# A selective-scan stage: stores of dl, of the C and B rows and of y begun by ScalarE instead of SyncE

## The reference, cut to what matters

```
x_dbl = einsum('bkdl,kcd->bkcl', xs, x_proj_w)      # 6 dt rows, 16 B rows, 16 C rows
delta = softplus(einsum(dts, dt_proj_w) + dt_proj_b) # 192 rows
dA = exp(delta[..., None] * A)                       # 192 channels x 16 states
h  = dA * h + (delta * u)[..., None] * B             # along the 4096 pixels
y  = einsum('bkdn,bkn->bkd', h, C)
return y + xs * Dk                                   # the four k are then added up
```

## Time and profile before

| | |
|---|---|
| time, median of 3 runs | 11577.95 us (11575.34 to 11589.02) |
| time of the profiled execution | 11574.58 us |
| its span, first to last instruction | 11572.8 us |
| granted TensorE clock, mean | 0.957 |
| DVE busy | 10116.4 us (87%) |
| ACT busy | 8511.6 us (74%) |
| POOL busy | 9157.8 us (79%) |
| data moved | 1716.32 MB |

### The profile page before, as it was taken

One profiled execution on the slowest core, in us unless ns is written; L12 is line 12 of the kernel. 1 busy time (PEld: TensorE's weight loads), 2 busy tenths in 40 slices (PEclk: granted clock), 3 DMA queues, 4 the chain that ended last, 5 costly groups with the idle time before them and its releaser, 6 DMA issues. The chain is left out here.

```text
span 11572.8 us, 332532 instructions
## 1 busy us (share of the span) xinstructions
PE 9678.0 (84%) x136268; PEld 6104.2 (53%) x136268; DVE 10116.4 (87%) x6303; ACT 8511.6 (74%) x15618; POOL 9157.8 (79%) x3978
## 2 busy tenths in 40 slices
PE   8967888788888788888787778888888887999999
PEld 5644444444444444444444444444444444788778
DVE  7879999999999999999999999999999996555554
ACT  3468888887888788878888888788888884444443
POOL 1169999998999899989999999899999996433330
PEclk9989999999999999999999999999999998999999
DMA  3366676676667766776677666666766674212210
GB/s 103 106 164 169 171 175 171 167 178 168 172 166 174 177 167 164 173 174 168 171 175 178 172 167 171 175 168 171 178 174 166 171 175 111 65 48 67 61 50 12
DMA packets 561649, 1716.32 MB, mean 148 GB/s; under 512 B 147138, under 2 KB 147938, under 8 KB 558344
## 3 DMA queue, kind: packets, MB, share of 16 engines
q1 hardware_dynamic: 560136, 1695.05, 58.4%
HBM read 1319.08 MB, written 375.39 MB: 146 GB/s over the span
## 5 line engine op out<-in xcount | busy, mean ns | idle before, releaser
L975 POOL TENSOR_TENSOR HC<-H,crep 128x1024 f32<-128x1024 f32 x3072 | 7201.2, 2376 | 583.8 <-PE psum L723 416.0
L797 DVE TENSOR_TENSOR_SCAN H<-E,car,psum 128x1024 f32<-128x1024 f32 x2112 | 4868.7, 2336 | 237.4 <-PE psum L701 113.3
L701 PE MATMUL psum<-diag,dluT 128*32 128x128 f32 x98304 | 3350.7, 288 | 1083.0 <-DVE H L797 1049.2
L701 PEld LDWEIGHTS psum<-diag,dluT 128*32 128x32 f32 x98304 | 2852.9, 116 | 2080.8 <-DVE H L797 1887.9
L882 ACT ACTIVATE E<-dlr,am 128x1024 f32<-128x1024 f32 x2816 | 3194.4, 1143 | 1001.7 <-DMA dlr<-scr_dl 519.4
L866 ACT ACTIVATE diag<-idn,blt 128x128 f32<-128x128 f32 x8192 | 2521.6, 389 | 119.8 <-PE psum L701 119.8
L723 PE MATMUL psum<-HC,sely 128*32 128x512 f32 x12288 | 2232.0, 620 | 32.6 <-POOL HC L975 30.9
L775 DVE TENSOR_TENSOR psum<-dur,psum 128x1024 f32<-128x1024 f32 x1280 | 1548.7, 1210 | 114.6 <-PE psum L664 90.4
L797 DVE TENSOR_TENSOR_SCAN H<-E,psum 128x1024 f32<-128x1024 f32 x704 | 1582.1, 2276 | 75.6 <-PE psum L701 45.9
L664 PE MATMUL psum<-sx,selb 96*128 96x512 f32 x2560 | 981.4, 465 | 532.4 <-DVE H L797 522.3
L664 PEld LDWEIGHTS psum<-sx,selb 96*128 96x128 f32 x2560 | 395.4, 190 | 1423.5 <-DVE H L797 1139.3
(11 more groups left out here) (143 smaller groups left out, 9796.9 us busy)
## 6 DMA issues: line engine op xcount, KB each, us to landing
dur<-scr_dlu SPq DMA_DIRECT2D x3072, 128.0 KB, 4.0
dlr<-scr_dl SPq DMA_DIRECT2D x3072, 128.0 KB, 3.8
crep<-scr_bc SPq DMA_DIRECT2D x1024, 256.0 KB, 5.2
scr_dlu<-dlu SPq DMA_DIRECT2D x256, 384.0 KB, 4.6
scr_yk<-yt SPq DMA_DIRECT2D x256, 384.0 KB, 3.0
brep<-scr_bc SPq DMA_DIRECT2D x512, 128.0 KB, 3.5
scr_dl<-dlt SPq DMA_DIRECT2D x128, 384.0 KB, 5.6
scr_dl<-yt SPq DMA_DIRECT2D x128, 384.0 KB, 3.3
```

What stands on the lines that cost most here:

```text
L701: r = e.matmul(P[un % 2][32 * q:32 * q + 32, i * 128:(i + 1) * 128], dluT[:, m % 2, i, 32 * j:32 * j + 32], diag[:, i, at + q, :], start=T ...
L797: e.tensor_tensor_scan(H[:, un % NH, ::step], decay[:, ::step], drive[:, ::step], init, ALU.mult, ALU.add).then_inc(scan_done)
L975: e.tensor_tensor(HC[:, un % NHC, :], H[:, un % NH, :], crep[:, GREP.index(g), :], ALU.mult).then_inc(hc_done)
```

## The change

The stores of delta, of the B and C rows and of y leave SyncE's order, and ScalarE begins them, at units written out in its loop: `store_y(n - 1)` at unit 5 of every step, `out_bc(c)` at unit 6 of an even step, `out_dl(2c)` at unit 8 and `out_dl(2c + 1)` at unit 11. Each stands behind the exponential that `ahead` issues at that unit. The functions are the same, with the same waits. The stores of dlu stay on SyncE.

```diff
@@ sync
-        def out_dl(m):
...
-        def out_bc(c):
...
-        def store_y(m):
...
                 if n:
                     in_crep(c - 1, 1)
-                    store_y(n - 1)
                 load_y(n + 1)
...
-                if c < NCHUNK:
-                    out_bc(c)
                 if more:
                     in_dlr(n + 1, 2)
                     in_dur(n + 1, 2)
...
                 if n + 2 < NSTEP:
                     out_dlu(n + 2)
-                    out_dl(n + 2)
-                    out_dl(n + 3)
             else:
...
                 if n + 2 < NSTEP:
                     out_dlu(n + 2)
-                store_y(n - 1)
                 load_y(n + 1)
@@ scalar
+        def out_dl(m):
+            if m >= 4:
+                for j in range(NJ):
+                    e.wait_ge(dlr_in[slot(m - 4, j)], loaded(m - 4, j))
+            e.wait_ge(dl_made, m + 1)
+            e.dma_start(S["dl"][m % 4], dl[m % 2]).then_inc(dl_out[m % 2], 16)
+
+        def out_bc(c):
+            if c >= 2:
+                e.wait_ge(crep_in[1], 64 * (c - 1))
+            e.wait_ge(bc_copied, c + 1)
+            e.dma_start(S["bc"][c % 2], bc[NR:NR + NS + 4, :]).then_inc(bc_out, 16)
+
+        def store_y(m):
+            b, k, ci, half = steps[m]
+            t0 = t_of(k, ci)
+            e.wait_ge(y_copied, m + 1)
+            e.dma_start(S["yk"][b, k % 2, half, :, t0:t0 + TC], yt[:]).then_inc(y_stored, 16)
...
             ahead(un)
+            if n < NSTEP and n % 2 == 0 and c < NCHUNK:
+                if x == 6:
+                    out_bc(c)
+                if x == 8:
+                    out_dl(2 * c)
+                if x == 11:
+                    out_dl(2 * c + 1)
+            if x == 5 and n:
+                store_y(n - 1)
             if un % 2 == 0 and has_carry(un - 1):
                 carry(un - 1)
```

More of the change, by code:

```diff
@@ L577, in sync @@
             load_rows(0, ci)
-        out_bc(0)
         for i in range(2):
@@ L582, in sync @@
         for m in range(2):
-            out_dl(m)
             out_dlu(m)
@@ L630, in sync @@
                     in_crep(c, 0)
-        store_y(NSTEP - 1)
         e.wait_ge(y_stored, 16 * NSTEP)
@@ L912, in scalar @@
         project(0)
+        out_bc(0)
         delta(0)
+        out_dl(0)
         turn_b(0)
@@ L916, in scalar @@
         delta(1)
+        out_dl(1)
         e.wait_ge(a_made, 2)
```

## The result

The changed kernel takes 11631.8 us (median of 6 runs, 11619.4 to 11661.6) against 11578.4 us (11571.1 to 11589.0) before it: a ratio of 1.0051, 95% interval 1.0037 to 1.0066. It is slower, by 53 us; 38 were forecast. The ratio is worked out from all runs, so it is not quite that of the two medians (1.0046); its interval is 43 to 76 us. The profiled execution has a span of 11617.6 us, 44.8 more than before. It is the fastest of the six, with a mean granted TensorE clock of 0.958, where the six together have 0.955; the runs of the kernel before that were timed beside the experiments have 0.958.

A forecast was written before the change was run, and what follows sets the result against it. VectorE was taken to bound the scan, its idle time set by the landing of dlr third 0. Losses of 14 us (lines one and two) and 24 us (three and four) gave 11578 + 38 = 11616 us, range 11551 to 11700.

The forecast's parts named there:

- What bounds the scan: Scan: the change acts through VectorE's idle time; dlr third 0's landing decides, and waits beyond about 3.4 us cost nearly fully.
- Point 2: First dl store, moved ahead of dlr third 0's landing: delays it 0.8 us; 14 us lost in lines one and two, 24 later.
- Point 1, the head start: Lines three and four: without bc ahead on SyncE, dlr loads start 0.42 us earlier per pair, gaining at most 27 us.
- Point 3: ScalarE's loop: issuing the stores is hidden under the exponentials and costs nothing; if not hidden, 0.6 us per pair.
- Point 4: Second dl store and y stores: moving them, and the earlier loads for step n + 2, give nothing.
- A: Rival, critical loads: not bound by the DMA engines, so the store is free; 11551 us, -0.23%; chance 0.14.
- B: Rival, dl store: price of 0.2 to 0.6 us, half covered by slack, no change to be told; 11564 to 11598 us; chance 0.26.
- C: Rival, ScalarE: store issue not hidden, 0.6 us more on the landing; 11675 us; chance 0.13.
- D: Rival, DMA engines: the dl store is paid at the loads' rate, 1.7 us; 11710 us; chance 0.10.
- The signs: Profile: ScalarE's dlr wait up 40 to 100 us, VectorE's busy time unchanged, SyncE's L573 and L535 waits about the same.
- a sum of 52 us: DMA queues taking turns packet by packet: the dl store's full price of 0.94 us is paid, 33 + 19 = 52 us.

The follow-up runs named there:

- the two runs with nothing in the way: Changed kernel with the first dl store back on SyncE, 11572.6 us, ratio 0.9991; or at unit 10 of ScalarE's loop, 11574.2 us, ratio 0.9993.
- the two other runs that lose as much: Kernel before with only the first dl store on ScalarE at unit 8, 11641.9 us; or with it ahead of dlr third 0 on SyncE, 11638.9 us.
- the late store: Changed kernel with the first dl store at unit 10 of ScalarE's loop in place of unit 8: 11574.2 us, ratio 0.9993.

## Why the prediction was right, point by point

- **What bounds the scan.** Right. VectorE's busy time is unchanged, and all of the loss is idle time: over the first seven images, in windows, the total grew by 41.0 us (7905.80 to 7946.84) and VectorE's busy time by 2.7 (7544.86 to 7547.56). The landing of dlr third 0 was the point on which it turned: well ahead of its use, it gives 106 us; delayed by one store, it takes 53.
- **Point 2, the price of the store.** Right in place and sign, a little small in size. It was priced at 0.8 us for the landing, and at 14 us in the first two lines and, less the head start, 24 in the last two. By the windows above, scaled to 64 pairs each, it was 0.21 x 64 = 13 us and 0.58 x 64 = 37 us. The wait grew by 87 us over 128 pairs, 0.7 us each: by 1.0 in the first two lines, where most of it was covered, and by 0.66 in the last two, where nearly all of it was paid (0.58 by the windows). So 0.8 was a good mean of two different delays; it was taken as the middle of 0 and 1.7, and that it came out so well is in part luck. The store was also begun earlier than the prediction has it: not right behind the exponential of unit 10 but ahead of its start, 7.85 us before the exponential of unit 12 in place of some 5.
- **Point 1, the head start.** Wrong: it was not there to be taken off in the last two lines. It was costed at 0.42 us for each of 64 pairs, 27 us in all. With the loss undone, the head start should show: the two runs with nothing in the way gave 7.5 and 5.9 us, both with an interval that reaches 1 and whose other end, 21 and 22 us, lies under 27. Timelines show why, SyncE's first and then ScalarE's, in a pair of a fourth line, in the run with one store put back, answering to the earlier trace rows:

```profile
4009.99 0.32 SPq L562 DMA_DIRECT2D yp<-scr_yk  x1
...
4010.88 1.83 SPq L519 DMA_DIRECT2D dlr<-scr_dl  x4
...
4024.76 1.15 ACT L862 ACTIVATE E<-dlr,am 128x1024 f32<-128x1024 f32 x1 [7.43 <-DMA dlr<-scr_dl]
```

  The dlr loads start 0.89 us after yp, where it was 1.31, but the exponential starts 14.77 us after yp, where it was 14.49. The same holds over all pairs. In the fourth lines the dlr loads start 1.31 us after yp before, and 0.89 in this run (medians of 32 pairs); in the third lines there was hardly a head start at all, 0.81 and 0.71. From yp to the exponential of unit 12 it is 13.77 us before and 13.72 in this run in the fourth lines, and 11.55 and 11.65 in the third (means). The step that failed read a head start in issue as one in landing. The likely reason: yp is in the queue ahead, and in the pair of the earlier trace rows the DMA engines are busy at a share of 0.97 to 1.09 from 4004 to 4016, so the landing goes by when they begin and by how many bytes there are, not by when SyncE writes the last of them.
- **What the prediction left out: TensorE's clock.** In the windows of images 2 to 7, last two lines, the clock stands at the lower of its two levels (0.5 of full speed) for 307 to 333 us in the three profiles with the loss and for 268 to 300 us in the three without. Over the lines of these six profiles, a us at the lower level goes with a line longer by 0.19 us. By this estimate some 0.1 of the 0.73 us per pair comes with the clock. Between single runs of the kernel before it shows too: 11560.6 us at a mean clock of 0.962 and 11605.7 at 0.953. That the longer waits lower the clock is not shown.
- **Point 3, ScalarE's time at nothing.** Right. The store is issued under a running instruction, and the run with all five stores on ScalarE and this one moved to unit 10 shows no loss.
- **Point 4, nothing from the rest.** Right within the error: putting back the first dl store alone brings back the time before.
- **The rivals.** A (the store is free) falls with the changed kernel and the two other runs that lose as much; but the 313 GB/s of loads and store together, against 243 to 254 of loads alone, shows that its mechanism works in part. B (nothing to be told) falls with the interval of 43 to 76 us. C falls with the late store. D would have asked for 132 us.
- **The signs.** ScalarE's wait rose by 87 us, within the 40 to 100 named. VectorE's work is unchanged. But the prediction had SyncE's waits for yp and for the exponential remain with about their totals, and they grew by 924 and 749 us: with the stores gone, SyncE reaches these waits earlier and stands there until the same moment.
- The Trainium skill (DMA: Bandwidth & Descriptors, "Issuing engines are not separate DMA queues") was cited for transfers of different engines that interleave on the same 16 DMA engines; the runs agree, 11641.9 us from ScalarE's queue and 11638.9 from SyncE's. The turn-taking between queues that this page of the Trainium skill states ("Queues, rings and completion order") fits the 142 GB/s of the store beside 171 of the loads. It gave a sum of 52 us where 53 were measured; but that agreement is partly luck, since that sum holds the head start, which was not there. And turns between queues are not needed for the loss: it is as large with all transfers in one queue.

## What to carry to other kernels

Moving the beginning of a transfer to another engine frees a queue, and with it the transfer's place in time. Before it is moved, find the load whose landing somebody waits for, and see what will then be in flight ahead of it: here one store of 384 KB, begun some 7 us earlier, cost 53 us, while ridding SyncE of some 2200 us of listed waits brought next to nothing. A long wait in a queue's listing is worth something only if what stands behind it is late; the cure was to move the critical load ahead of the waits, one line of code for 0.9%.

## What the runs showed of the hardware that was not expected

- A transfer begun by ScalarE took 0.32 us in its instruction stream, and was issued under the running instruction, here the table load: at 2093.05, 1.2 us before the exponential that stands in front of it in the program started at 2094.25.
- A share of about 1.0 on the DMA engines does not mean one rate: 243 to 254 GB/s (means by line) with loads of 32 partitions each, 313 while a store took turns with them, 418 in the one window of the earlier trace rows with stores alone. Why the loads are slower was not tried.
- With the DMA engines at that share, loads begun 0.42 us earlier in the same queue let the exponential that needs them start no earlier than by 0.05 us (13.72 us after yp in place of 13.77, means of the fourth lines).
